# Latent attention with a gated feed-forward: moving a subtraction to GpSimd and a rope addition to ScalarE

## What is computed

```python
xn = layernorm(x)
q = (xn @ wq).reshape(b, s, 16, 192)               # 128 nope, 64 rope
ckv, k_pe = split(xn @ wkv_a)                      # 64 and 64
ckv = rmsnorm(ckv) * kv_norm_scale
k_nope, v = split((ckv @ wkv_b).reshape(b, s, 16, 256))
scores = concat(q_nope, rope(q_pe)) . concat(k_nope, rope(k_pe)) * 192 ** -0.5
attn = softmax(where(causal, scores, min))
s = (attn @ v) @ wo
g = silu(ffn(xn))       # silu(gate) * up, then down; inner width 704
x = x + s * g
```

## Time and profile before

| | us |
|---|---|
| median of 3 runs | 1127.04 (1126.23 to 1129.42) |
| the profiled execution | 1129.4 |
| its span | 1127.6 |
| granted TensorE clock, mean | 0.955 |

### The profile page before, as it was taken

How to read it: one execution, slowest core, us unless ns; L and a number is a source line. 1 busy time by engine, 2 the same in 40 slices (tenths; PEclk the granted TensorE clock), 3 DMA queues, 4 the chain that set the end, 5 groups by cost and what they waited for, 6 DMA issues and landing times.

```text
span 1127.6 us, 26426 instructions
## 1 busy us (share of the span) xinstructions
PE 975.5 (87%) x10560; PEld 835.3 (74%) x10560; DVE 894.6 (79%) x1383; ACT 734.8 (65%) x1061; POOL 674.3 (60%) x448
## 2 busy tenths in 40 slices
PE   5658898889897989898998889898989898779998
PEld 5536777777786868776877777777778686668887
DVE  5757988897989898889888888888898889772134
ACT  1327786777667867777777777687768686662232
POOL 3655957584849484848485757666675657522332
PEclk7869999999999999999999999999999999899999
DMA  5019999999999999999999998999999899992001
GB/s 164 9 47 173 175 185 156 180 158 180 160 178 159 176 172 178 169 166 171 170 166 167 174 168 165 170 174 163 187 158 182 156 169 199 181 182 75 1 20 57
DMA packets 591979, 170.24 MB, mean 151 GB/s; under 512 B 574064, under 2 KB 585968, under 8 KB 591856
## 3 DMA queue, kind: packets, MB, share of 16 engines
q1 hardware_dynamic: 587376, 167.89, 83.5%
q10 hardware_dynamic: 4480, 0.66, 0.4%
HBM read 15.41 MB, written 2.10 MB: 16 GB/s over the span
## 4 chain that ended last, share of the span: by engine, by line
DVE 19%; PE 19%; issue 7%; SPq 6%; POOL 5%; ACT 3%; DMA 1%; ACTq 0%; POOLq 0%
DVE hl L938 8%; PE s_ps L523 8%; PE s_ps L621 5%; DVE part_max L929 4%; DVE neg_max L927 3%; SPq L459 2%; PE slot_ps L523 2%; SPq L466 2%; POOL hl L1097 2%; PE o_ps L523 2%; POOL pe L1097 1%; DVE acc L901 1%; SPq L453 1%; ACT hl L726 1%; DVE pe_b L886 1%
## 5 line engine op out<-in xcount | busy, mean ns | idle before, releaser
L789 ACT ACTIVATE prob<-s_ps,neg_max 128x1024 f32<-128x1024 f32 (+7 forms) x384 | 318.6, 865 | 209.1 <-DVE neg_max L927 122.2
L1097 POOL TENSOR_TENSOR hl<-prob,hl 128x1024 f16<-128x1024 f32 x128 | 288.3, 2252 | 238.1 <-ACT hl L726 235.5
L929 DVE TENSOR_REDUCE part_max<-s_ps 128x1 f32<-128x1024 f32 (+7 forms) x256 | 244.2, 984 | 80.5 <-PE s_ps L621 66.9
L726 ACT ACTIVATE hl<-prob 128x1024 f16<-128x1024 f32 (+7 forms) x384 | 296.4, 806 | 7.1 <-DMA pT<-hl 5.7
L637 PE MATMUL o_ps<-v,pT 128*128 128x65 f16 x2176 | 232.1, 194 | 65.6 <-DVE o_tiles L950 62.3
L938 DVE TENSOR_TENSOR hl<-prob,hl 128x768 f16<-128x768 f32 (+7 forms) x256 | 279.6, 1132 | 4.5 <-ACT hl L726 2.2
L637 PEld LDWEIGHTS o_ps<-v,pT 128*128 128x128 f16 x2176 | 206.5, 98 | 71.2 <-issue 67.4
L638 PE MATMUL o_ps<-v,pT 128*128 128x64 f16 x2176 | 232.6, 197 | 0.0
L639 PE MATMUL o_ps<-v,pT 128*128 128x65 f16 x2176 | 231.6, 193 | 0.0
L639 PEld LDWEIGHTS o_ps<-v,pT 128*128 128x128 f16 x2176 | 205.9, 100 | 0.0
L638 PEld LDWEIGHTS o_ps<-v,pT 128*128 128x128 f16 x2176 | 205.2, 98 | 0.0
(11 more groups left out here) (183 smaller groups left out, 1994.2 us busy)
## 6 DMA issues: line engine op xcount, KB each, us to landing
q_swap<-q_pe SPq DMA_DIRECT2D x128, 64.0 KB, 2.0
pT<-hl SPq DMA_TRANSPOSE x256, 4.8
wq_sb<-in_L_attn_wq_dram SPq DMA_DIRECT2D x8, 384.0 KB, 4.2
acc<-in_L_attn_x_dram SPq DMA_DIRECT2D x4, 512.0 KB, 6.6
wo_sb<-in_L_attn_wo_dram SPq DMA_DIRECT2D x8, 256.0 KB, 3.2
x_in<-in_L_attn_x_dram SPq DMA_DIRECT2D x1, 2048.0 KB, 8.3
out_dram<-y SPq DMA_DIRECT2D x8, 256.0 KB, 2.1
wkvs<-in_L_attn_wkv_b_dram SPq DMA_DIRECT2D x8, 128.0 KB, 4.1
```

Of the source, the lines that this page charges most:

```text
L726: return nc.scalar.activation(dst, src, ACT.Copy)
L789: nc.scalar.activation(prob_of(u, m), score_bank(u, m), ACT.Exp, bias=neg_max[:, r:r + 1]).then_inc(exp_done, 1)
L929: nc.vector.tensor_reduce(part_max[:, u % 2, m:m + 1], src, AX.X, ALU.max).then_inc(part_done, 1)
L1097: return lambda: nc.gpsimd.tensor_tensor(dst, a, b, op)
```

## The change

Four things. GpSimd also makes the low half of the narrower of spans 1 and 2 (`smaller`: 128, 256, 384, 512, 512, 384, 256, 128 columns in steps 0 to 7), as its last step of each unit, `rest`; VectorE keeps the wider one. `rope_of_b` goes to ScalarE as a copy; GpSimd's step 2 adds both halves. `normalise` runs once for the two units of a step, on four columns of sums, with `o_ps` holding both heads side by side. `q_pe` and `q_swap` have two buffers, so that a group waits for the one two before it.

```diff
+def smaller(u):
+    return 2 if step_of(u) < HALF // 2 else 1
...
-POOL = Steps(POOL_SETUP + [name for u in range(NU) for name in [("low", u)] + steps_at(u)])
+POOL = Steps(POOL_SETUP + [name for u in range(NU) for name in [("low", u)] + steps_at(u) + [("rest", u)]])
...
@@ SP, swap
-                if n >= 1:
-                    before = GROUP_ORDER[(n - 1) % NG], (n - 1) // NG
+                if n >= 2:
+                    before = GROUP_ORDER[(n - 2) % NG], (n - 2) // NG
                     sp.wait_ge(pool_done, POOL.after((f"rope{before[0]}.2", before[1])))
-                    sp.wait_ge(rope_b, n)
@@ SP, turn_rest
-                sp.wait_ge(lo_dve, 2 * u + 2)
+                sp.wait_ge(lo_dve, u + 1)
+                sp.wait_ge(pool_done, POOL.after(("rest", u)))
@@ PE, weigh
-                if m == 0 and u >= 1:
-                    pe_eng.wait_ge(norm_done, u)
+                if m == 0 and head_of(u) == 0 and u >= 2:
+                    pe_eng.wait_ge(norm_done, u // 2)
...
-                c0 = (LORA + 1) * (m // 2)
+                c0 = (LORA + 1) * (2 * head_of(u) + m // 2)
@@ ACT, query jobs
-                    if n >= 1:
-                        act.wait_ge(swapped, 64 * n)
+                    if n >= 2:
+                        act.wait_ge(swapped, 64 * (n - 1))
@@ ACT, between the jobs and the high halves of spans 1 and 2, k = 4, 6, 12, 14
+            def rope_of_b(g, pair):
+                n = group_no(g, pair)
+                act.wait_ge(pool_done, POOL.after((f"rope{g}.2", pair)))
+                if n >= 2:
+                    before = GROUP_ORDER[(n - 2) % NG], (n - 2) // NG
+                    act.wait_ge(pool_done, POOL.after((f"B{before[0]}lo", before[1])))
+                copy(pe_b[:, n % 2, :], pe[ROPE:P, n % 2, :]).then_inc(rope_b, 1)
@@ ACT, exponentials
                 elif m > 0 and u >= 2:
-                    act.wait_ge(lo_dve, 2 * (u - 2) + 2)
+                    act.wait_ge(lo_dve, u - 1)
+                    act.wait_ge(pool_done, POOL.after(("rest", u - 2)))
@@ DVE
-                nc.vector.tensor_tensor(pe_b[:, n % 2, :], pe[ROPE:P, n % 2, :], q_swap[ROPE:P, :], ALU.add).then_inc(rope_b, 1)
...
-                if u >= LAG + 1:
+                if u >= LAG + 1 and head_of(u - LAG - 1) == 1:
                     normalise(u - LAG - 1)
...
-                    prob_low(u, 1)
-                    prob_low(u, 2)
+                    prob_low(u, 3 - smaller(u))
@@ POOL
-                    run((name, pair), tt(turned[0:ROPE, :], turned[0:ROPE, :], q_swap[0:ROPE, :], ALU.add))
+                    run((name, pair), tt(turned, turned, q_swap[:, n % 2, :], ALU.add))
...
             for u in range(NU):
-                prob_low(u)
+                prob_low(u, 0)
                 for name in steps_at(u):
                     step(name)
+                prob_low(u, smaller(u))
```

More of the change, by code:

```diff
@@ L247, in mla_gated_ffn_kernel @@
         sinT = ab("sinT", [P, S])
-        q_pe = ab("q_pe", [P, BANK])
-        q_swap = ab("q_swap", [P, BANK])
+        q_pe = ab("q_pe", [P, 2, BANK])
+        q_swap = ab("q_swap", [P, 2, BANK])
         pe = ab("pe", [P, 2, BANK])
@@ L316, in mla_gated_ffn_kernel @@
         neg_max = ab("neg_max", [P, 4])
-        rinv = ab("rinv", [P, 2, 2])
+        rinv = ab("rinv", [P, 2, 4])
         attn.close()
@@ L446, in swap @@
                 n = group_no(g, pair)
-                if n >= 1:
-                    before = GROUP_ORDER[(n - 1) % NG], (n - 1) // NG
+                if n >= 2:
+                    before = GROUP_ORDER[(n - 2) % NG], (n - 2) // NG
                     sp.wait_ge(pool_done, POOL.after((f"rope{before[0]}.2", before[1])))
-                    sp.wait_ge(rope_b, n)
                 for i in range(4):
                     a, b = slice(i * half, (i + 1) * half), slice((i ^ 1) * half, (i ^ 1) * half + half)
-                    sp.dma_start(q_swap[a, :], q_pe[b, :]).then_inc(swapped, 16)
+                    sp.dma_start(q_swap[a, n % 2, :], q_pe[b, n % 2, :]).then_inc(swapped, 16)
             def turn_first(u):
@@ L567, in out_job @@
                 if name.startswith("outT"):
-                    pe_eng.wait_ge(norm_done, pair * PU + 4 * q + 4)
+                    pe_eng.wait_ge(norm_done, (pair * PU + 4 * q + 4) // 2)
                     for j in range(BLK):
@@ L704, in down @@
                 if n == 0:
-                    pe_eng.wait_ge(norm_done, NU)
+                    pe_eng.wait_ge(norm_done, NU // 2)
                 for tp in range(2):
@@ L745, in prep_job @@
                     n = group_no(g, pair)
-                    if n >= 1:
-                        before = GROUP_ORDER[(n - 1) % NG], (n - 1) // NG
-                        act.wait_ge(swapped, 64 * n)
+                    if n >= 2:
+                        before = GROUP_ORDER[(n - 2) % NG], (n - 2) // NG
+                        act.wait_ge(swapped, 64 * (n - 1))
                         act.wait_ge(pool_done, POOL.after((f"rope{before[0]}.0", before[1])))
-                    copy(q_pe[h * ROPE:(h + 1) * ROPE, :], ps[0:ROPE, :])
+                    copy(q_pe[h * ROPE:(h + 1) * ROPE, n % 2, :], ps[0:ROPE, :])
                     if pair > 0:
@@ L812, in _ @@
                     prep_job(*name)
+                if name == ("qA0", 0):
+                    rope_of_b(3, 0)
+            rope_of_b(0, 0)
             for u in range(NU + 1):
@@ L821, in _ @@
                 if u < NU:
+                    pair, k = divmod(u, PU)
+                    if k in ROPE_B_OWN:
+                        rope_of_b(ROPE_B_OWN[k], pair)
+                    if k in ROPE_B_NEXT and pair < PAIRS - 1:
+                        rope_of_b(ROPE_B_NEXT[k], pair + 1)
                     prob_high(u, 1)
@@ L941, in normalise @@
                 pair, k = divmod(u, PU)
-                head = head_of(u)
-                o = o_ps[:, 0:2 * (LORA + 1)].rearrange("p (t c) -> p t c", t=2)
+                n = u // 2
+                o = o_ps[:, 0:4 * (LORA + 1)].rearrange("p (h t c) -> p h t c", h=2, t=2)
+                r = rinv[:, n % 2, :].rearrange("p (h t) -> p h t", h=2)
                 dve.wait_ge(pv_done, scores_through(u))
-                nc.vector.reciprocal(rinv[:, u % 2, :], o[:, :, LORA]).then_inc(recip_done, 1)
-                dve.wait_ge(recip_done, u + 1)
+                nc.vector.reciprocal(r, o[:, :, :, LORA]).then_inc(recip_done, 1)
+                dve.wait_ge(recip_done, n + 1)
                 q, j = divmod(k // 2, 2)
-                if k % 4 == 0 and (q >= 2 or pair > 0):
+                if j == 0 and (q >= 2 or pair > 0):
                     dve.wait_ge(slot_ready, after("ready", (f"outT{(q - 2) % NG}", pair - (q < 2))))
-                nc.vector.tensor_tensor(o_tiles[:, q % 2, 2 * j:2 * j + 2, head * LORA:(head + 1) * LORA],
-                                        o[:, :, 0:LORA], rinv[:, u % 2, :].unsqueeze(2).to_broadcast([P, 2, LORA]), ALU.mult).then_inc(norm_done, 1)
+                nc.vector.tensor_tensor(o_tiles[:, q % 2, 2 * j:2 * j + 2, :].rearrange("p t (h c) -> p h t c", h=2), o[:, :, :, 0:LORA],
+                                        r.unsqueeze(3).to_broadcast([P, 2, 2, LORA]), ALU.mult).then_inc(norm_done, 1)
             def stats(n):
@@ L1030, in _ @@
             values_and_keys(2)
-            rope_of_b(3, 0)
             split_first(3)
@@ L1038, in _ @@
             query_lo(("qB0", 0))
-            rope_of_b(0, 0)
             split_first(0)
@@ L1119, in rope_step @@
                     done = ((queries_split, n - 1),) if 2 <= n < 4 else ()
-                    run((name, pair), tt(turned, q_pe[:], cosT[:, query_cols(g)], ALU.mult), (hi_done, after("hi", (f"qB{g}", pair))),
+                    run((name, pair), tt(turned, q_pe[:, n % 2, :], cosT[:, query_cols(g)], ALU.mult), (hi_done, after("hi", (f"qB{g}", pair))),
                         (tables_loaded[g], 32), *done)
                 elif i == 1:
-                    run((name, pair), tt(q_swap[:], q_swap[:], sinT[:, query_cols(g)], ALU.mult), (swapped, 64 * (n + 1)))
+                    run((name, pair), tt(q_swap[:, n % 2, :], q_swap[:, n % 2, :], sinT[:, query_cols(g)], ALU.mult), (swapped, 64 * (n + 1)))
                 else:
-                    run((name, pair), tt(turned[0:ROPE, :], turned[0:ROPE, :], q_swap[0:ROPE, :], ALU.add))
+                    run((name, pair), tt(turned, turned, q_swap[:, n % 2, :], ALU.add))
             def split_step(name, pair):
@@ L1160, in step, with prob_low @@
                     split_step(*name)
-            def prob_low(u):
-                both = halves_of(u, 0)
-                run(("low", u), tt(both[:, W0:2 * W0], prob0[:], both[:, 0:W0], ALU.subtract), (prob_hi, scores_through(u, 0)))
+            def prob_low(u, m):
+                w = width(u, m)
+                both = halves_of(u, m)
+                run(("rest" if m else "low", u), tt(both[:, w:2 * w], prob_of(u, m), both[:, 0:w], ALU.subtract), (prob_hi, scores_through(u, m)))
```

## The result

The changed kernel takes 1120.94 us (median of 6, 1119.44 to 1123.3) against 1128.39 (6 runs, 1126.23 to 1131.52): ratio 0.9932, 95% interval 0.9913 to 0.995. It is faster, by 7.5 us where I had forecast 35. The profiled execution took 1121.3 us, span 1119.5.

What follows compares the result with a forecast made beforehand. It took VectorE (k = 4 to 7, 11 to 13) and TensorE (k = 0 to 2, 8 to 10) as bounds. Terms summed to -5.5 us a pair, -34.5 in all, from 1127.04 to 1092 us, own range 1080 to 1105.

Steps and rivals of the forecast that it cites:

- What bounds it: Per head pair: TensorE bounds units 0 to 2 and 8 to 10, VectorE units 4 to 7 and 11 to 13.
- k = 4 to 7: Units 4 to 7 of a head pair: GpSimd becomes the bound, 29.6 us against 28.99, 0.6 us longer.
- k = 0 to 2: Units 0 to 2 of a head pair, TensorE-bound: 0.2 us shorter.
- k = 8 to 10: Units 8 to 10 of a head pair: TensorE enters without its backlog, 1.9 us shorter, between 0 and 2.6.
- k = 11 to 13: Units 11 to 13 of a head pair: GpSimd has nothing to wait for, 22.0 us against 22.59, 0.6 shorter.
- k = 3: Unit 3 of a head pair: GpSimd's swap wait stays about 1.5 us; 9.0 us against 9.44, 0.4 shorter.
- k = 14 and 15: Last two units of a head pair: shorter chain to the exponential, 12.8 us against 15.83, 3.0 shorter (1.5 to 4).
- ScalarE's stall of 3.04 us: In k = 3, ScalarE's wait before copying rope rows, from the single q_pe/q_swap: goes, but GpSimd becomes ready only as late.
- Rival 1: Little gain: VectorE's remaining wide subtraction is served strictly in turn with GpSimd's; 1110 us (1103 to 1120), chance 0.20.
- Rival 2: More gain: VectorE was the only cause and TensorE takes over; 1065 us (1058 to 1080), chance 0.15.
- Rival 3: Slower: transposed spans 1 and 2 reach TensorE late, in eight units a pair; 1155 us, chance 0.12.
- Rival 4: No change: the DMA engines set the pace; 1127 us, chance 0.08.

Runs made afterwards that it cites:

- e2: Changed kernel with the narrow subtraction back on VectorE, the other three parts kept: 1072.34 us, ratio 0.9477.
- e3: Kernel before with the two q_pe/q_swap buffers alone: 1098.17 us, ratio 0.9724.
- e1: Changed kernel with SP issuing a unit's four swap DMAs ahead of the transposition of span 0: 1097.65 us, ratio 0.9715.
- e7: Kernel before with two rope buffers and head B's rope addition as a ScalarE copy; normalisation per unit, both subtractions on VectorE: 1066.93 us, ratio 0.9435.
- e4: Changed kernel with a single q_pe/q_swap buffer again: 1131.34 us, ratio 1.0007.
- e10: Changed kernel with both low halves on VectorE and, in place of GpSimd's narrow subtraction, a memset of about the same length: 1113.81 us, ratio 0.9867.
- e5: Changed kernel with the narrow subtraction back on VectorE and the swap DMAs first: 1066.44 us, ratio 0.9434.
- e8: As e5, next pair's weights loaded in k = 12, narrow subtraction on GpSimd only in k = 0 to 2, 8 to 10, 14, 15: 1064.27 us, 0.9411.
- e12: As e7, with the swap DMAs first and the next pair's load in k = 12 instead of k = 0: 1061.96 us, ratio 0.9411.

## Why the prediction went wrong

- *What bounds it* was right for k = 4 to 7 (VectorE) and for k = 0 to 2 and 8 to 10 (TensorE, busy all through). For k = 11 to 13 VectorE is not shown to be the bound: e2 takes the addition off it, and the stretch is 23.72 us against 22.59, with 3.2 us of waiting for the swap in it. The removal in k = 4 to 7 came as forecast: VectorE 21.01 us busy (21.1 forecast), GpSimd 28.29 of 29.86 (near 28 of 29.6 forecast). Over the pair VectorE lost 16.4 us, not 21, since its wide subtractions lengthened.
- *k = 0 to 2, 3, 4 to 7, 8 to 10, 14 and 15* were forecast at -0.2, -0.4, +0.6, -1.9 and -3.0 and came out at +0.6, -0.4, +0.9, -1.2 and -3.6: together -3.7 where I had -4.9. Over the six middle pairs they average -4.9 together, which is partly luck, for k = 8 to 10 (-2.6) and k = 0 to 2 (+0.6) miss in opposite directions.
- *k = 11 to 13* is the step that failed: "with a relief of up to 0.5 and nothing to wait for, 22.0 against 22.59". Measured 25.38, +2.8 (+3.3 over the middle pairs), with a wait of 3.12 us for the swapped rows in it. I had seen for k = 3 that the swap is late from SP's queue, and had let that wait stay; for k = 11 I let its 1.5 us of before vanish. It doubled, because SP's queue did not get faster with the stretch ahead: in e2 and e3, where k = 8 to 10 are faster too, the wait is 3.2 and 3.3 us. e1 takes most of it out, and the stretch falls to 23.53. The first pair repeats the miss: 1.2 us longer, where I had it 3 shorter.
- That e1 saves 32 us on the kernel before, close to the 35 that I had forecast, is a coincidence. Nearly half of what e1 gains is the wait in k = 3, which my sum had let stay, and even in e1 k = 11 to 13 is 1.5 us above my 22.0, with GpSimd busy 21.80.
- *The narrow subtraction.* I called 0.6 us in k = 4 to 7 "what speaks against the change", measured from the kernel before. Its price is what the kernel would be without it: 29.86 against e2's 26.44 in that stretch, 51 us in all. I had credited it with VectorE's relief, 4.7 us of 7.4 there; e2 and e7 show that the additions' 2.2 were enough to let VectorE through, and what comes off VectorE beyond that is worth nothing while GpSimd is the bound.
- *The buffers.* "ScalarE's stall of 3.04 us goes, but GpSimd becomes ready only as late": true with the narrow subtraction in GpSimd's queue, where it then hides; false without it, 31 us (e3). e4 shows that even beside it they are worth 8 us. I had also counted the stall once in a pair, and it is there twice, 3.04 us in k = 3 and 2.12 in k = 11, as 14 waits in seven pairs could have told me. ScalarE's row of k = 11, before:

```profile
512.11 0.59 ACT L726 ACTIVATE q_pe<-slot_ps 64x512 f32<-64x512 f32 x1 [2.12 <-issue]
```

- *Rival 1* (little gain) named the result, within its 1103 to 1120 but for one us, though not by its mechanism: GpSimd's subtraction of span 0 took 2150 ns on average, less than the 2252 of before, and k = 4 to 7 came within 0.3 us of the sum without the rival. VectorE's wide subtractions were the ones to lengthen, from 986 to 1729 ns on average, by width, to 1407 to 1791. My sum against this rival was wrong, though: its 25.8 for GpSimd holds the time for which VectorE held GpSimd up. At each form's shortest time the sixteen steps take 21.8, and 21.8 and 5.7 would fit into the 28.99 one behind the other.
- What the Trainium skill says in Perfetto Trace Analysis (Optimizing Scalar/DVE Operations), that such a move might not help, came true, but the port that the two engines share does not make the price: e10's memsets leave VectorE alone and cost 44 us.
- *Rival 2* (TensorE takes over, 1058 to 1080) has the time that e2 and e5 to e8 reach, once GpSimd is spared the narrow subtraction where its queue is full. *Rival 3* did not come: TensorE's waits for pT rose from 3 to 12 us. *Rival 4* was partly right: the transposition queue is full in k = 8 to 10, and sets when the swap lands, but not the pace: e12 makes the same transpositions in 59 us less.

Not settled: how the 31 us of the buffers divide. They shortened stretches (k = 14 and 15) that hold no stall of ScalarE.

## What to carry to other kernels

Price each part of a change against the kernel with the other parts in, not against the kernel before: here two parts gave 64 us and a third took some 50 of them back, and the sum looked like a small success. Work moved to an engine that idles on average (GpSimd 60%) costs in full in the stretches where its queue is full; look at its share there first. And where a stretch gets faster, ask what small DMA stands behind large ones in the same queue, for it is now late.

## What the runs showed of the hardware

A subtraction on VectorE is held up by an operation on GpSimd that reads two tensors, and not by a memset: 768 columns take 1778 ns on average beside the one, 945 beside the other and 948 with GpSimd idle (e10).

SP's issue of one and the same transposition (span 0's, 2048 columns) took from 1.81 us to 3.25 us within 10 us of the changed kernel, that of spans 1 and 2 from 2.74 to 4.21, almost without a pause between them: the time that an issue takes is no property of the transfer alone. A memset on GpSimd of 1260 uint8 columns takes 1.15 us, about as long as a subtraction of 512 columns (1.26).
